# One order of pieces for odd and one for even steps, with maxima, scores and exps as single units, in the fused step of an sLSTM, attention and mixture-of-experts layer on one core

## The reference

```python
x = x + _L0_attn_ref(_layernorm(x, axis=-1), W, b, input_bias, scale)
x = x + _L0_ffn_ref(_layernorm(x, axis=-1), w_qkv, w_o, g1, b1, wg, w1, bb1, w2, bb2, g2, b2)
```

## Time and profile before

| | us |
|---|---|
| median of the runs | 1213.33 |
| lowest and highest of 3 runs | 1212.72 and 1230.21 |
| the profiled execution | 1221.32 |
| its span, first to last instruction | 1219.6 |
| TensorE busy in the span | 985.7 (81%) |
| VectorE busy | 888.4 (73%) |
| ScalarE busy | 716.9 (59%) |
| GpSimd busy | 598.4 (49%) |

### The profile page before, as it was taken

One profiled execution on the slowest core, in us unless ns is written; L12 is line 12 of the kernel. 1 busy time (PEld: TensorE's weight loads), 2 busy tenths in 40 slices (PEclk: granted clock), 3 DMA queues, 4 the chain that ended last, 5 costly groups with the idle time before them and its releaser, 6 DMA issues. The chain is left out here.

```text
span 1219.6 us, 26342 instructions
## 1 busy us (share of the span) xinstructions
PE 985.7 (81%) x7237; PEld 762.0 (62%) x7237; DVE 888.4 (73%) x2573; ACT 716.9 (59%) x1740; POOL 598.4 (49%) x797
## 2 busy tenths in 40 slices
PE   1457889889889889889888898977169999999865
PEld 1236566666566566666566666654059999999721
DVE  4457778877888888878889787665737777777558
ACT  3654667766766766666577554444145656565546
POOL 6200244433466456456475747556715655555600
PEclk9977899988999999998899998897579999999979
DMA  1024433433433433342442444323223333333177
GB/s 48 1 80 112 96 77 96 96 81 87 100 91 108 100 94 105 91 115 70 114 113 72 113 104 120 99 67 83 87 71 98 86 96 83 95 87 86 29 204 211
DMA packets 137973, 114.70 MB, mean 94 GB/s; under 512 B 19314, under 2 KB 126456, under 8 KB 137860
## 3 DMA queue, kind: packets, MB, share of 16 engines
q1 hardware_dynamic: 120772, 92.24, 29.8%
q0 software_dynamic: 8640, 16.93, 4.3%
q10 hardware_dynamic: 8448, 4.20, 1.2%
HBM read 60.60 MB, written 52.58 MB: 93 GB/s over the span
## 5 line engine op out<-in xcount | busy, mean ns | idle before, releaser
L1010 DVE TENSOR_REDUCE b_m_neg<-b_ps_m 128x2 f32<-128x512 f32 (+1 forms) x384 | 246.8, 683 | 44.4 <-PE b_ps_m L1343 24.8
L741 ACT ACTIVATE b_PT<-b_ps_s 128x512 f32<-128x512 f32 x384 | 216.0, 599 | 86.5 <-PE b_ps_s L1330 58.9
L593 POOL TENSOR_SCALAR_AFFINE_SELECT b_PT<-b_PT 128x256 f32<-128x256 f32 (+1 forms) x384 | 184.1, 504 | 151.0 <-ACT b_PT L741 150.1
L1630 POOL DMA_INDIRECT results<-e_Y,e_X x142 | 149.6, 1054 | 123.6 <-DVE e_Y L1697 100.3
L610 POOL DMA_INDIRECT slots<-c_pay,b_pos x128 | 132.4, 1034 | 31.8 <-issue 26.3
L1745 PE MATMUL e_ps_d<-e_h,e_w 128*128 128x256 f32 x568 | 135.0, 381 | 0.0
L1330 PE MATMUL b_ps_s<-c_QK 128*128 128x512 f32 x256 | 111.9, 437 | 22.8 <-ACT b_PT L741 22.6
L1350 PE MATMUL b_ps_m<-c_QK 128*128 128x256 f32 x512 | 118.8, 337 | 0.0
L1657 ACT ACTIVATE e_h<-e_ps,e_w 128x256 f32<-128x256 f32 x284 | 111.3, 480 | 0.8 <-PE e_ps L1736 0.8
L1745 PEld LDWEIGHTS e_ps_d<-e_h,e_w 128*128 128x128 f32 x568 | 102.9, 191 | 11.2
L1347 PE MATMUL b_ps_m<-mask_b,ident_b 128*128 128x256 bf16 x256 | 75.2, 294 | 32.1 <-DVE b_m_neg L1010 29.7
(11 more groups left out here) (242 smaller groups left out, 2502.4 us busy)
## 6 DMA issues: line engine op xcount, KB each, us to landing
c_QK<-qk_scr SPq DMA_DIRECT2D x128, 192.0 KB
qk_scr<-b_qk_hi SPq DMA_DIRECT2D x64, 256.0 KB, 2.7
e_X<-slots SPq DMA_DIRECT2D x71, 130.0 KB, 2.3
qk_scr<-b_qk_lo SPq DMA_DIRECT2D x32, 256.0 KB, 2.9
f_G<-results SPq DMA_DIRECT2D x32, 256.0 KB, 4.1
a_X<-in_L_attn_x_dram SPq DMA_DIRECT2D x16, 256.0 KB, 6.6
x<-a_X SPq DMA_DIRECT2D x16, 256.0 KB, 3.5
b_X<-x SPq DMA_DIRECT2D x32, 128.0 KB, 6.0
```

Of the source, the lines that this page charges most:

```text
L593: nc.gpsimd.affine_select(out=tri, in_=tri, compare_op=ALU.is_ge, fill=0.0, base=0, pattern=[[0, tri.shape[1]], [1, P]], channel_multiplie ...
L741: nc.scalar.activation(PT[:, g % 2, u], ps_s[:, (3 * g + u) % 2], ACT.Exp, scale=HD ** -0.5).then_inc(s_e, 1)
L1010: nc.vector.tensor_reduce(out, scores, AX.X, ALU.max, negate=True).then_inc(s_red, 1)
L1630: nc.gpsimd.indirect_dma_start(dram["results"][:, :], bass.IndirectOffsetOnAxis(X[:, j.of(NB_X), u, D:D + 1].bitcast(u32), 0), Y[:, n, u, ...
```

## The change

The same arithmetic is done on the same tiles and buffers; the pieces stand in another order. What changes:

1. The helpers handle single units: `maximum(b, u)`, `score(c, q)`, `exp(b, q)`, `reduce(b, u)`. `cell_gates` becomes three pieces (i, o, z), `residual` splits into sum, statistics and means, `rows_stats` and `rows_means` stand apart.
2. `step` of TensorE, ScalarE, VectorE and GpSimd has two written-out orders, one for odd and one for even s. SyncE's step is untouched.
3. The waits follow the new positions, with the same semaphores and the same number of buffers (two halves of `ps_m`, two of `ps_s`, two groups of `PT`, three of `QK`).

The core of the new TensorE and VectorE orders for even steps:

```diff
@@ tensor, def step(s), even s
-                    if C:
-                        scores(c, 0, (0, 1))
-                    if B1:
-                        maxima(b1, 6, 8)
-                    if C:
-                        scores(c, 0, (2,))
-                    if PP:
-                        values(p, 3)
-                    if gf.exists(GROUPS):
-                        cell_turn(gf)
-                    if B1:
-                        maxima(b1, 8, 10)
...
+                    score(c, 0)
+                    score(c, 1)
+                    maximum(b1, 6)
+                    values(p, 3)
+                    score(c, 2)
+                    score(c, 3)
+                    maximum(b1, 7)
+                    maximum(b1, 8)
+                    cell_turn(gf)
+                    score(c, 4)
+                    o_rows(p, 1)
+                    maximum(b1, 9)
+                    score(c, 5)
+                    values(c, 0)
+                    score(c, 6)
+                    maximum(b1, 10)
+                    rows_turn(a, p)
...
@@ scalar, def step(s), even s
+                    exp(c, 0)
+                    exp(c, 1)
+                    cell_rows(gf)
+                    exp(c, 2)
+                    evac_o(p, 1)
+                    exp(c, 3)
+                    cell_high(gf)
...
@@ vector, def step(s), even s
+                    cell_shift(gf)
+                    cell_gated(gi)
+                    route_first(routed)
+                    reduce(b1, 6)
+                    cell_norm(gi)
+                    reduce(b1, 7)
+                    rows_norm(a)
+                    route_rest(routed)
+                    reduce(b1, 8)
+                    cell_low(gf)
+                    reduce(b1, 9)
...
@@ gpsimd, def step(s), odd s
+                    sends(s, 0)
+                    sends(s, 1)
+                    mask(c, 0)
+                    sends(s, 2)
+                    mask(c, 1)
+                    cell_forget(gh)
+                    rows(d)
+                    sends(s, 3)
+                    mask(c, 2)
+                    mask(c, 3)
```

More of the change, by code:

```diff
@@ new lines, in step @@
+                    exp(c, 1)
+                    evac_o(p, 1)
+                    exp(c, 2)
+                    exp(c, 3)
+                    cell_rms(gj)
+                    root_out(q)
+                    exp(c, 4)
+                    hidden(r)
+                    rows_high(a)
+                    exp(c, 5)
+                    maxima_row(b1)
+                    route_gap(routed)
+                    exp(c, 6)
+                    cell_input(gh)
+                    logits(r)
+                    attended(p)
@@ L1128, in tables, with rows_norm @@
                 nc.vector.tensor_scalar(kept["tile_at"][:, :], tile_f[:, 2, :], float(E * REGION), None, ALU.min)
+            def rows_norm(a):
+                if not a.exists(B):
+                    return
+                k, x = a.of(NB), a.of(NX)
+                need(dve, s_rstd, a + 1)
+                for t in range(2):
+                    last = nc.vector.tensor_scalar(XN[:, k, t, :], X[:, x, t, :], mv[:, t, 0:1],
+                                                   rstd[:, t:t + 1], ALU.subtract, ALU.mult)
+                last.then_inc(s_xn, 1)
@@ new lines, in hidden_norm, with rows_low @@
+            def hidden_norm(q):
+                if not q.exists(B):
+                    return
+                need(dve, s_rstd1, q + 1)
+                need(dve, s_h1, q)
+                for t in range(2):
+                    last = nc.vector.tensor_scalar(H0[:, t, :], R[:, t, :], mv1[:, t, 0:1],
+                                                   rstd1[:, t:t + 1], ALU.subtract, ALU.mult)
+                last.then_inc(s_h0, 1)
+            def rows_low(a):
+                if not a.exists(B):
+                    return
+                need(dve, s_xhi, a + 1)
+                nc.vector.tensor_tensor(xt_lo[:, :], ps_x[:, 1, 0:T], xt_hi[:, :].bitcast(fp32), ALU.subtract).then_inc(s_xlo, 1)
@@ L1354, in values @@
+                done.then_inc(s_b, 1)
             def values(c, g):
+                if not c.exists(B):
+                    return
                 n = c.of(NV)
@@ new lines, in columns @@
+            def columns(a):
+                if not a.exists(B):
+                    return
+                need(pe, s_xlo, a + 1)
+                for i in range(2):
+                    w, out = slice(i * D, (i + 1) * D), ps_x[:, 1, i * T:(i + 1) * T]
+                    nc.tensor.matmul(out, w_lo[:, w], xt_hi[:, :], start=True, stop=False)
+                    nc.tensor.matmul(out, w_hi[:, w], xt_lo[:, :], start=False, stop=False)
+                    last = nc.tensor.matmul(out, w_hi[:, w], xt_hi[:, :], start=False, stop=True)
+                last.then_inc(s_qk, 1)
```

884 lines of the change are left out of this document (531 added, 353 removed).

## The result

The changed kernel takes 1106.4 us (median of 4 runs, 1105.7 to 1111.1), the kernel before on the same chip 1218.4. The ratio is 0.908 with a 95% interval of 0.900 to 0.916: faster by 9%, 112 us. The forecast was 1160, with a range from 1128 to 1206. The sign was right, the size half of what came.

What follows compares the result with a forecast made beforehand. In-order queues whose heads wait for one another were taken as the bound. Plain pairs of 41.0 us gain 48 with routing and half clock, later steps 8: 1221.3 becomes 1165, less 5 is 1160 us; range 1128 to 1206.

Steps and rivals of the forecast that it cites:

- The floor of 38.6: TensorE's busy time in a plain pair of steps, 38.6 us, taken as the least a pair can take.
- Chains around `cell_turn` and `cell_low`: Even steps: TensorE's waits of 1.43 us before the `a_XN` transposes and 1.60 for reductions shrink to 0.2 each.
- Exps (0.7 left): TensorE's waits for exps, 1.8 us per pair before, of which 0.7 was kept as remaining.
- New waits from the singles (+1.3): Cost of 1.3 us per pair for tight places and units standing alone, whose late weights lose 0.2 us each.
- Routed pairs: Pairs with routing: VectorE's 41.2 us plus 2.3 of its own waits, 43.5 us, 2.5 over plain.
- The 8 later steps: Steps without the recurrence, 20.4 us each before, taken as 19.4 after: a gain of 8 us.
- The reload: Rival: loading QK again between steps becomes the bound, each step ending 1.5 us later, 1202 us in all; chance 0.10.
- The ramp: Ramp up of batches before the first stretch, bound by each batch's own chain: gain 0.
- GpSimd: Odd steps: `cell_forget` and `rows` stand ahead of masks 2 and 3; nothing in the sum, up to 2 us in the range.
- The port: SBUF port shared by VectorE and GpSimd: the loss moves from `rows_norm` to `hidden_norm` and `cell_input`, about 1 us per pair.
- The slower rival: Each unit handed over alone exposes a 0.44 us wait, 20 of 48 per pair: 1263 us; chance 0.09.
- no order helps: Rival: TensorE's waits are what semaphores between engines cost in any order, so 1213 us; chance 0.09.

Runs made afterwards that it cites:

- e9: Changed kernel, with reductions from a step's fifth unit on reading only half of their input (work left out): 1096.0 us, ratio 0.894.
- e1: Kernel before, with four pieces moved in even steps (ScalarE's cell_rows and cell_high, TensorE's cell_turn, VectorE's cell_low): 1196.4 us, ratio 0.973.
- e4: Changed kernel with both new orders, but maxima, reductions, scores and exps kept in pairs: 1140.3 us, ratio 0.927.
- e14: Changed kernel with only the maxima matmuls and their reductions in pairs again: 1141.8 us, ratio 0.919.
- e2: Kernel before, with the new order on all four engines in even steps only: 1176.3 us, ratio 0.955.
- e11: Changed kernel with GpSimd's move of cell_forget in odd steps undone, so it stands ahead of the first group's mask again: 1159.5 us, ratio 0.946.
- e7: Changed kernel with VectorE's route_rest, route_second and route_marks moved earlier in odd steps: 1099.6 us, ratio 0.903.
- e13: Kernel before with only GpSimd's cell_forget moved in odd steps, behind the second group's mask: 1304.3 us, ratio 1.047.
- e3: Kernel before, with the new order on all four engines in odd steps only: 1206.0 us, ratio 0.983.

## Why the prediction was right in sign and wrong in size

The time lies 22 us below the range's end. The bound and its chain were read rightly; what failed is what was kept as loss. Three terms did it: the ramp, put at nothing (20 us came), the waits left in the pairs, among them a cost for single units that turned out a gain (18.5 us more than forecast), and the later steps (17.3 more). They failed in one direction, and one opposite error, in the routed pairs, hid 13.6 us of the second. Step by step:

- **The bound: right.** In-order queues whose heads wait held the kernel, and with them gone TensorE is full (38.0 of 38.2 us).
- **The floor of 38.6: 0.6 too high.** The same work is 38.0 in the changed kernel, 37.8 in e9. Why 0.6 us less is open: single matmuls are as long as before (score matmuls of the maxima 322 ns in the mean in both pairs).
- **Chains around `cell_turn` and `cell_low`: right.** 0.2 us each was forecast to be left; nothing is left of the first wait, TensorE's waits for reductions before maxima are 3.1 us in 8 times instead of 21.7 in 19, and e1 shows both chains as a gain of some 33 us.
- **Exps (0.7 left): too high.** Four waits of 7.5 us in all over 11 pairs, none in a plain pair.
- **New waits from the singles (+1.3): wrong sign.** In this step the mechanism failed, not only a size. e4 and e14 show the singles as a gain, of 21 us up to step 35 in e4, most of it from the maxima. The step took a unit that stands alone as 0.2 us lost for late weights (the earlier trace rows against the earlier trace rows), for some of the 18 or so, and added a few tight places; it gave the singles no gain. In the changed kernel TensorE had other work between two units, and its waits for reductions all but went; that this other work let a reduction free its half of `ps_m` in time is argued from the orders. The four residual terms made 2.4 us per plain pair; measured are 0.2 (38.19 - 38.01). With 0.6 for the floor that is 2.8 us per pair, 31 for 11 pairs; 18.5 of them came as gain beyond the forecast, and the next line has the rest.
- **Routed pairs: right in length.** 43.5 was forecast; 25.25 + 18.6 = 43.9 came. Over the shorter plain pair that is 5.7 (four times; 3.3 in the last), where the sum had 2.5 five times: 13.6 us more, which is why the pairs together were only 18.5 off.
- **Half clock in the pairs (2.5 us left of 8): about right.** The granted clock of the first stretch is 0.98, as forecast; 17.1 us of it are at 1.2 GHz instead of 44.4. What they cost was not measured apart.
- **The 8 later steps: 8 forecast, 25 measured.** I kept them at 19.4 us each; they took 17.2. TensorE's busy time there fell by 14.5 us with the same matmuls, the clock going from 0.88 to 0.95; the other 11 are idle time. The loss stands in the earlier trace rows (22.8 us idle, clock 0.88), and the 1 us per step of the sum was not worked out from it. The reload, one of the rivals, does show there (6.1 us), and nowhere in the 22 steps.
- **The ramp: 0 forecast, 20 measured.** The argument was that each batch's own chain binds it. But the order of the pieces sets the length of that chain too: with the even order alone it was 10.6 us shorter (e2), with both 18.6 (e4). TensorE's waits there fell from 20.7 to 14.5 us for `a_XN` and from 7.2 to 3.3 for `a_z`; the rest of the 19.9 was not traced.
- **GpSimd: nothing in the sum, and a wrong reason.** Nothing was lost, as the sum had it, but by luck: e11 shows that 50 us hang on the place of `cell_forget`. The step asked for room on GpSimd, where there was plenty, and not when `a_M` is made in the new order.
- **The port (a loss of about 1 us per pair that moves): right.** `cell_input`'s `a_i_s` took 1.74 us in the median of the 11 pairs instead of 0.68, `rows_norm` lost its long ones (at most 0.80 instead of 1.30), and VectorE's busy time in a plain pair is 36.2 us (36.5 before). Not foreseen were the small routing operations; below.

The spans differ by 115.6 us, the sum gave 56. Of the 59.6 between them 19.9 are the ramp, 18.5 the pairs, 17.3 the later steps and 3.8 the tail. The slower rival (singles that each expose a wait) is refuted by e4 and by the waits after; "no order helps" by the result; of the reload, 6.1 us in the later steps is all that came from step 5 on.

## What to carry to other kernels

On in-order queues a piece has no good place by itself: ask of each moved piece when its input is made and who stands behind its result, on all three queues; one GpSimd product was worth +58 us in one order and -50 in the other, with half of that engine's time idle. And count the stretches of the same loop that one did not look at: ramp and later steps gave 45 of the 116 us by which the spans differ.

## What was not expected of the hardware

- **Small VectorE operations beside GpSimd.** The two rows above at 251.25 and 257.05 are the same form on 128x64, 1.28 and 0.21 us. GpSimd's and VectorE's rows beside them:

```profile
251.19 1.27 POOL L582 TENSOR_TENSOR a_f_s<-a_M,a_sp 128x512 f32<-128x512 f32 x1
252.54 1.18 POOL L584 TENSOR_TENSOR a_f_s<-a_M,a_f_s 128x512 f32<-128x512 f32 x1
...
257.03 1.36 POOL L607 TENSOR_TENSOR c_pay<-b_H,b_b 128x512 f32<-128x512 f32 x1
```
```profile
257.29 1.18 DVE L1188 TENSOR_TENSOR b_MK<-b_M 128x64 bf16<-128x64 f32 x1
```

  The long ones do not take a fixed multiple: 251.25, 252.57 and 257.29 each start while a GpSimd product runs and end within 0.1 us of its end (252.53 and 252.46, 253.79 and 253.72, 258.47 and 258.39). The one at 257.05 starts with the product, within 0.02 us, and is not held. The Trainium skill, "SBUF — State Buffer", Who interferes with whom, says that a VectorE instruction with two SBUF inputs contends with a GpSimd instruction that reads SBUF, and that of two such the second to issue waits for the first to finish. The trace agrees for these three, which have two such inputs each (L1188 adds two parts of `b_M`). e7, told above, shows that what is moved out of one product can fall into the next.
- **The half clock around short waits.** TensorE's wait of 1.82 us that ends at 256.06 stands at the start of the first stretch at 1.2 GHz since step 5 (the second row; before it the clock was full for 164 us):

```profile
249.00:255.60 6.60, 5.14 (x48) 3.88 (x47) 6.50 (x14) 2.43 (x8) 3.37 (x5) 1.00 0.02 5
255.60:262.40 6.80, 6.34 (x42) 4.99 (x42) 6.70 (x25) 3.69 (x12) 3.50 (x5) 0.50 0.09 29
```

  Over steps 5 to 35 the trace has 84.8 us at the half clock before, 30.7 after, 194.3 in e13. A wait can thus cost more than its own length: the plain pair of e11 has 3.1 us more idle and 2.9 more busy. But not every one does: e14, with 14 waits for exps and 11 for `a_XN` of up to 1.1 and 1.4 us, has only 10.2 us at the half clock, less than the changed kernel. Which waits bring it on, no run here separates.
- **The tail differs between groups.** Unchanged code took 10 to 26 us longer in two of the groups (35 in the executions of e1 and e3), and by 12 us more in one kernel than in another on one chip; the cause is open. A version compared across groups by its median alone would have been misjudged by as much.
